# Denominator in two float32r parts from the second image on, with two-segment instructions, in a windowed-similarity kernel

## The chip, the cores and the metric

The kernel runs on one core of one Trainium2 chip. The metric is the device time of one execution in microseconds. The engines are TensorE (PE, with its weight loads shown as PEld), VectorE (DVE), ScalarE (ACT), GpSimd (POOL) and SyncE (SP), which here issues all the DMAs. All data are float32.

## What is computed

Two layers act on x of shape (2 images, 256 rows, 256 columns, 384 channels). Each layer normalises x by groups of 12 channels and adds a ratio of windowed sums (window 5 along the image's width, 20 along the channels):

```python
def layer(x):
    x_n = _gn(x)                              # G = 32, mean and variance over (H, W, C // G)
    s = box_sum(x_n, 2, 5)                    # width window
    num = box_sum(s * s, 3, 20)               # channel window
    d = box_sum(box_sum(x_n * x_n, 2, 5), 3, 20)
    denum = d * c1[None, None, :, None]       # c1: how many columns each width window holds
    return x + nan_to_num(num / denum, nan=1.0)
out = layer(layer(x))
```

The statistics of a layer's input must be known before the layer may begin on that image.

## The kernel before

The work falls into four phases, `PHASES`: layer 1 image 1, layer 1 image 2, layer 2 image 1, layer 2 image 2. The notes below and the prediction call them phases 0 to 3. A phase has 128 pairs of image rows (`NPAIR`), a tile has 8 rows (4 pairs), and a loop body has two tiles (8 pairs, `BODY`). Two `x_in` and two `y_out` buffers hold one tile each. One pair is four segments (`PSEG`) of 128 columns by 384 channels.

What each engine does for a pair p:

- POOL: `centre` (L312) subtracts the mean, two pairs ahead; `add_ratio` (L321) adds x to the finished ratio of the pair before.
- ACT: `squares` (L369, two halves, `Q0` and `Q1`); `take` (L385 and L388) moves a width sum out of PSUM, squared for the numerator (`sT`, steps `S`), copied and scaled for the denominator (`tT`, steps `T`); `invert` (L398 and L401, steps `L0` to `L3`) makes a reciprocal of a denominator segment as Exp(-Ln(d)).
- PE: `width_unit` (L468) multiplies the centred values (`S0` to `S2`) and the squares (`T0` to `T2`) by the width band, four matmuls of 130 output columns for each of three channel blocks, into three `width_ps` banks taken in turn. `channel_unit` (L492) multiplies `tT` (`D0` to `D3`, into three `den_ps` banks) or `sT` (`N0` to `N3`, into two `num_ps` banks) by the channel band, three matmuls of 138, 147 and 137 columns for each segment. In both the data are the stationary operand, so that each matmul in the code has a weight load.
- DVE: `approach` (L631) and `weigh` (L637) for each of the four segments, `divide` (L649) once for the pair (together one Newton step and the product), `measure_output` (L555, eight BATCH_NORM_STATS2 for each pair in phases 0 and 1, for layer 2's statistics) and `measure_beside` (L555, in phase 0, statistics of image 2: 3, 3 and 5 instructions in three of four pairs). `lane_totals` (L562) aggregates at a few places, eight or eleven instructions at a time.
- SP: for each tile the load of the tile after next, the store of the finished one, and in phase 0 the tile for `measure_beside`.

The order on each engine is written out by hand. PE works through the list below for each pair, where S and T belong to the next pair and D and N to the current one (F are three short parts in which the next phase's statistics are made, once in a phase). ACT's list is `S0 L0 T0 L1 S1 Q0 T1 L2 Q1 S2 T2 L3`. DVE's order is the body of `tiles`. Nothing reorders these lists, and an instruction that waits holds up all that stands behind it on its engine.

```python
for what in ("S0", "F1", "D0", "F2", "T0", "D1", "S1", "F3", "N0", "T1", "D2", "S2", "N1", "T2",
             "D3", "N2", "N3"):
```

Of the kernel before, what the change touches and what calls it, by code (L numbers as in the profile page):

```python
# [25 lines left out]
F32 = mybir.dt.float32  # L26
ACT = mybir.ActivationFunctionType
# [18 lines left out]
def similarity_layers_kernel(nc, x, out):  # L46
# [27 lines left out]

    def tiles_of(t, b):
        return t[b].rearrange("h (j p) c -> p (h j) c", p=P)
# [5 lines left out]
    with ExitStack() as ctx:  # L82
# [14 lines left out]
        newton = sb("newton", [P, PSEG, C])  # L97
        beside = sb("beside", [P, SEGS, C])
# [11 lines left out]
        band_c = [sb(f"band_c{k}", [P, c_span[k][1] - c_span[k][0]]) for k in range(KB)]  # L110
        identity = sb("identity", [P, P])
# [23 lines left out]
        width_taken = sem("width_taken")  # L135
        den_done = sem("den_done")
# [49 lines left out]
        with nc.Block() as block:  # L186
# [161 lines left out]
            def _(act):  # L348
# [13 lines left out]
                def squares(ph, p, par, half):  # L362
                    if half == 0:
                        act.wait_ge(rows_centred, ph * NPAIR + p + 1)
                        if not is_opening(ph, p, 2):

                            act.wait_ge(width_done, (ph * NPAIR + p - 1) * UNITS)
                    h = slice(half * 2, half * 2 + 2)
                    nc.scalar.activation(square[par][:, h, :], centred[par][:, h, :], ACT.Square  # L369
                                         ).then_inc(rows_squared, 1)  # L370

                def take(ph, p, par, k, is_t):

                    u = 2 * k + is_t
                    if u == 0:
                        if isinstance(p, int) and p == 0:

                            act.wait_ge(params_ready, ph + 1)
                        if not is_opening(ph, p, 2):

                            act.wait_ge(num_done, (ph * NPAIR + p - 1) * PSEG)
                    act.wait_ge(width_done, (ph * NPAIR + p) * UNITS + u + 1)
                    src = width_ps[u % 3][:]
                    if is_t:
                        nc.scalar.activation(tT[par][:, k, :], src, ACT.Copy, scale=rvar_col[ph][:, k:k + 1]  # L385
# [5 lines left out]
                def invert(ph, p, par, i):  # L391

                    base = ph * NPAIR
                    if i == 0 and not is_opening(ph, p, 2):

                        act.wait_ge(ratio_done, base + p - 1)
                    act.wait_ge(den_done, (base + p) * PSEG + i + 1)
                    nc.scalar.activation(recip[par][:, i, :], den_ps[i % 3][:, 0:C], ACT.Ln, bias=bias_ln[:],  # L398
                                         scale=LN_SCALE).then_inc(log_done, 1)
                    act.wait_ge(log_done, (base + p) * PSEG + i + 1)  # L400
                    nc.scalar.activation(recip[par][:, i, :], recip[par][:, i, :], ACT.Exp, bias=bias_exp[:],  # L401
                                         scale=-1.0).then_inc(recip_done, 1)

                def step(ph, p, par):

                    (ph1, p1), (ph2, p2) = in_phase(ph, p + 1), in_phase(ph, p + 2)
                    for what in ("S0", "L0", "T0", "L1", "S1", "Q0", "T1", "L2", "Q1", "S2", "T2", "L3"):
                        n = int(what[1])
                        if what[0] == "L":
                            invert(ph, p, par, n)  # L410
                        elif what[0] == "Q":
                            if ph2 < NP_:
                                squares(ph2, p2, par, n)
                        elif ph1 < NP_:
                            take(ph1, p1, 1 - par, n, int(what[0] == "T"))

                finish_logs(0)
                for p in range(2):
                    for half in range(2):
                        squares(0, p, p, half)  # L420
# [11 lines left out]
            def _(pe):  # L432
# [4 lines left out]
                def finish_part(ph, part):  # L437
# [3 lines left out]
                    if part < 3:  # L441
                        for half in range(2):
                            last = nc.tensor.matmul(num_ps[part - 1][:, 0:GROUPS], over_p[:],  # L443
                                                    stat_two[:, 2 * (part - 1), half, :],
                                                    start=(half == 0), stop=(half == 1))
                    else:
                        for k in range(KB):
                            last = nc.tensor.transpose(den_ps[2][:, P * k:P * (k + 1)],
# [3 lines left out]
                def width_unit(ph, p, par, k, is_t):  # L452
# [4 lines left out]
                    if u == 1:  # L457
                        pe.wait_ge(rows_squared, (ph * NPAIR + p + 1) * 2)
                    if not (is_opening(ph, p, 1) and u < 3):
# [4 lines left out]
                    bank = width_ps[u % 3]  # L464
# [8 lines left out]
                def channel_unit(ph, p, par, i, is_num):  # L473

                    seg = (ph * NPAIR + p) * PSEG + i
                    if i == 0 and not is_num:

                        pe.wait_ge(width_taken, (ph * NPAIR + p + 1) * UNITS)
                    if is_num:
                        bank, data = num_ps[i % 2], sT[par]  # L480
                        if not (is_opening(ph, p, 1) and i < 2):

                            pe.wait_ge(num_used, seg - 1)
                    else:
                        bank, data = den_ps[i % 3], tT[par]
                        if not (is_opening(ph, p, 1) and i < 3):

                            pe.wait_ge(den_used, seg if i == 0 else seg - 2 if i == 3 else seg - 3)
                    at = (i // 2) * W + (i % 2) * P
                    for k in range(KB):  # L490
                        lo, hi = c_span[k]
                        last = nc.tensor.matmul(bank[:, lo:hi], data[:, k, at:at + P], band_c[k][:],  # L492
# [272 lines left out]
```

## Time and profile before

| | us |
|---|---|
| median of 3 runs | 6088.27 |
| lowest and highest run | 6087.27, 6088.81 |
| span of the profiled execution | 6085.2 |
| PE busy | 5723.6 |
| ACT busy | 5014.0 |
| DVE busy | 4144.7 |
| POOL busy | 3546.7 |
| start of the first width matmul | 323.3 |

The first 311 us make the statistics of image 1 on DVE, with PE idle. From 323 us on PE runs, and the four phases follow one another without a break. The phase boundaries lie, by PE's work, near 1792, 3226 and 4656 us. Matmuls are pipelined, so the pitch from the start of one unit to the start of the next is its cost in a full stream, and the duration shown for one matmul is longer than that. On ACT and DVE too the next instruction may start some 0.1 us before the end of the one ahead of it.

### The profile page before, as it was taken

Reading aid. Unit: us, or ns where it says so; the run is one execution under the profiler, and the core shown is the slowest. Engines: PE = TensorE matmul, PEld = TensorE weight load, DVE = VectorE, ACT = ScalarE, POOL = GpSimd, SP = SyncE. Lnnn points to the kernel's source line nnn. Section 1 sums busy time; section 2 is a strip of 40 time slices with the busy share of each in tenths; the row PEclk is TensorE's granted clock in tenths of the full one; section 3 lists DMA queues with packets and bytes.
Section 4 is the critical chain, followed back from the end, with each engine's and each line's share of the span. In section 5 each row is a group of like instructions: output and inputs, shape, how many; then the busy total and the mean of one; then the engine's idle time right before and its main releaser. Section 6 shows DMA issues by size and latency. Waiting matters only on the chain.

```text
span 6085.2 us, 139173 instructions
## 1 busy us (share of the span) xinstructions
PE 5723.6 (94%) x49196; PEld 5710.7 (94%) x49196; DVE 4144.7 (68%) x9033; ACT 5014.0 (82%) x8201; POOL 3546.7 (58%) x1043
## 2 busy tenths in 40 slices
PE   0089999999999999999999999999999999999999
PEld 0089999999999999999999999999999999999999
DVE  9988889988877766767667555555555555555555
ACT  0078888888888888888888888888888888888888
POOL 0056665566556666666665666666666666666665
PEclk9999999999999999999999999999999999999999
DMA  9946655556633433434334344343434434343343
GB/s 367 367 157 212 223 207 191 207 203 215 220 125 125 151 138 134 156 124 153 137 135 147 132 147 143 129 160 124 159 130 141 149 124 165 124 153 137 135 154 124
DMA packets 660641, 1007.81 MB, mean 166 GB/s; under 512 B 5168, under 2 KB 660528, under 8 KB 660528
## 3 DMA queue, kind: packets, MB, share of 16 engines
q1 hardware_dynamic: 660528, 1006.65, 47.1%
q14 instruction: 85, 0.70, 0.0%
q8 instruction: 28, 0.46, 0.0%
HBM read 603.98 MB, written 402.65 MB: 165 GB/s over the span
## 4 chain that ended last, share of the span: by engine, by line
PE 89%; DVE 8%; issue 2%; ACT 1%; DMA 0%; SPq 0%; DVEq 0%; POOL 0%; POOLq 0%; ACTq 0%
PE width_ps L468 43%; PE den_ps L492 23%; PE num_ps L492 23%; DVE out_stats L555 3%; DVE lane_mv L562 2%; DVE y_out L649 1%; DVE newton L631 1%; DVE recip L637 0%; DMA y_out<-in_x_dram 0%; DVE beside_stats L555 0%; ACT recip L398 0%; ACT recip L401 0%; SPq L198 0%; DVEq L555 0%; PE num_ps L443 0%
## 5 line engine op out<-in xcount | busy, mean ns | idle before, releaser
L312 POOL TENSOR_TENSOR centred<-x_in,mean_row 128x1536 f32<-128x1536 f32 x512 | 1771.0, 3459 | 1415.0 <-PE width_ps L468 1097.5
L321 POOL TENSOR_TENSOR y_out<-x_in,y_out 128x1536 f32<-128x1536 f32 x512 | 1771.4, 3460 | 1117.1 <-DVE y_out L649 1117.1
L631 DVE SCALAR_TENSOR_TENSOR newton<-den_ps,recip 128x384 f32<-128x384 f32 x2048 | 1110.7, 553 | 1884.7 <-ACT recip L401 1854.8
L492 PE MATMUL den_ps<-band_c,tT 128*128 128x138 f32 (+2 forms) x12288 | 1809.0, 283 | 9.6 <-DVE newton L631 9.6
L492 PE MATMUL num_ps<-band_c,sT 128*128 128x138 f32 (+2 forms) x12288 | 1732.6, 284 | 20.4 <-DVE recip L637 20.1
L468 PE MATMUL width_ps<-band_w,centred 128*128 128x130 f32 x12288 | 1628.3, 275 | 0.5 <-DVE rvar_col L620 0.5
L468 PE MATMUL width_ps<-band_wc,square 128*128 128x130 f32 x12288 | 1625.5, 275 | 0.0
L492 PEld LDWEIGHTS den_ps<-band_c,tT 128*128 128x128 f32 x12288 | 1608.9, 190 | 13.3 <-DVE newton L631 11.8
L492 PEld LDWEIGHTS num_ps<-band_c,sT 128*128 128x128 f32 x12288 | 1580.5, 190 | 27.7 <-DVE recip L637 22.9
L388 ACT ACTIVATE sT<-width_ps,rstd_col 128x512 f32<-128x512 f32 x1536 | 1035.8, 674 | 592.9 <-PE width_ps L468 592.9
L468 PEld LDWEIGHTS width_ps<-band_w,centred 128*128 128x128 f32 x12288 | 1507.0, 191 | 0.9 <-DVE rvar_col L620 0.9
L468 PEld LDWEIGHTS width_ps<-band_wc,square 128*128 128x128 f32 x12288 | 1504.1, 191 | 0.0
L401 ACT ACTIVATE recip<-recip,bias_exp 128x384 f32<-128x384 f32 x2048 | 1260.4, 615 | 66.5
L398 ACT ACTIVATE recip<-den_ps,bias_ln 128x384 f32<-128x384 f32 x2048 | 1183.1, 578 | 64.7 <-PE den_ps L492 16.6
L637 DVE SCALAR_TENSOR_TENSOR recip<-num_ps,recip 128x384 f32<-128x384 f32 x2048 | 1085.0, 547 | 0.1
L385 ACT ACTIVATE tT<-width_ps,rvar_col 128x512 f32<-128x512 f32 x1536 | 1040.3, 677 | 2.6 <-PE width_ps L468 2.6
L649 DVE SCALAR_TENSOR_TENSOR y_out<-newton,recip 128x1536 f32<-128x1536 f32 x512 | 903.4, 1764 | 22.9
L369 ACT ACTIVATE square<-centred 128x768 f32<-128x768 f32 x1024 | 848.9, 829 | 3.7 <-POOL centred L312 3.7
L555 DVE BATCH_NORM_STATS2 out_stats<-y_out 128x192 f32 (+1 forms) x2560 | 689.7, 344 | 1.2 <-DMA y_out<-in_x_dram 1.0
L443 PE MATMUL num_ps<-stat_two,over_p 128*128 128x32 f32 x32 | 6.0, 319 | 313.7 <-DVE stat_two L584 312.8
L443 PEld LDWEIGHTS num_ps<-stat_two,over_p 128*128 128x128 f32 x32 | 5.4, 241 | 314.6 <-DVE band_wc L578 311.6
L555 DVE BATCH_NORM_STATS2 beside_stats<-beside 128x192 f32 (+1 forms) x960 | 273.6, 345 | 0.2
(44 smaller groups left out, 302.8 us busy)
## 6 DMA issues: line engine op xcount, KB each, us to landing
x_in<-in_x_dram SPq DMA_DIRECT2D x80, 3072.0 KB, 11.0
first_layer_out<-y_out SPq DMA_DIRECT2D x64, 3072.0 KB, 18.2
x_in<-first_layer_out SPq DMA_DIRECT2D x64, 3072.0 KB, 10.9
out_dram<-y_out SPq DMA_DIRECT2D x63, 3072.0 KB, 18.1
beside<-in_x_dram SPq DMA_DIRECT2D x30, 3072.0 KB, 11.0
y_out<-in_x_dram SPq DMA_DIRECT2D x18, 3072.0 KB, 24.4
out_dram<-y_out SPq DMA_DIRECT2D x4, 768.0 KB, 3.5
```

The costliest lines, as they stand in the source:

```text
L312: nc.gpsimd.tensor_tensor(centred[e % 2][:], x_in[slot][:, g * PSEG:(g + 1) * PSEG, :], mean_row[ph % 2][:].unsqueeze(1).to_broadcast([P, ...
L321: nc.gpsimd.tensor_tensor(y_out[slot][:, g * PSEG:(g + 1) * PSEG, :], x_in[slot][:, g * PSEG:(g + 1) * PSEG, :], y_out[slot][:, g * PSEG:( ...
L385: nc.scalar.activation(tT[par][:, k, :], src, ACT.Copy, scale=rvar_col[ph][:, k:k + 1]).then_inc(width_taken, 1)
L388: nc.scalar.activation(sT[par][:, k, :], src, ACT.Square, scale=rstd_col[ph][:, k:k + 1]).then_inc(width_taken, 1)
L398: nc.scalar.activation(recip[par][:, i, :], den_ps[i % 3][:, 0:C], ACT.Ln, bias=bias_ln[:], scale=LN_SCALE).then_inc(log_done, 1)
L401: nc.scalar.activation(recip[par][:, i, :], recip[par][:, i, :], ACT.Exp, bias=bias_exp[:], scale=-1.0).then_inc(recip_done, 1)
L468: last = nc.tensor.matmul(bank[:, at:at + WN], data[:, r * 2 + j, P * k:P * (k + 1)], band[:, j, :], start=(r == 0 and j == 0), stop=(r == ...
L492: last = nc.tensor.matmul(bank[:, lo:hi], data[:, k, at:at + P], band_c[k][:], start=(k == 0), stop=(k == KB - 1), skip_group_check=True)
L555: last = nc.vector.bn_stats(stats[:, g, bass.ds(column * 6, 6)], tile[:, :, CG * g:CG * (g + 1)])
L631: nc.vector.scalar_tensor_tensor(newton[:, i, :], den_ps[i % 3][:, 0:C], TINY, recip[par][:, i, :], ALU.add, ALU.mult).then_inc(den_used, 1)
L637: nc.vector.scalar_tensor_tensor(recip[par][:, i, :], num_ps[i % 2][:, 0:C], TINY, recip[par][:, i, :], ALU.add, ALU.mult).then_inc(num_us ...
L649: nc.vector.scalar_tensor_tensor(y_out[slot][:, g * PSEG:(g + 1) * PSEG, :], newton[:], 2.0, recip[e % 2][:], ALU.subtract, ALU.mult).then ...
```

## The change

From phase 1 on (`SPLIT_FROM = 1`) the denominator's width sums are kept as two float32r tensors. ACT's `take` writes `t_top` (L385's place), a value rounded to float32r. A new DVE instruction, `rest`, computes the sum once more from the same PSUM bank and subtracts `t_top`, which gives `t_rest`. PE multiplies both by a float32r band, so that a D unit has six matmuls in the code in place of three. The band's spans begin on even columns: 138, 148 and 138 columns. Phase 0 keeps `tT` and its float32 band. Further:

- `width_ps` has two banks, one for S and one for T. T units wait for `rest` of the T unit before them (`rest_taken`).
- `den_ps` has two pairs of banks and `num_ps` one pair. `invert`, `approach` and `weigh` take two segments in one instruction, and `squares` takes the whole pair. ACT's list becomes `S0 T0 L0 S1 T1 Q S2 T2 L1`.
- `newton` is gone; `approach` writes into `y_out`, and so it now waits for the store of the earlier tile (`out_landed`), which `divide` did.
- D2 and N1 change places in PE's list.
- The new tensors take the memory of `beside`, which is not used after phase 0.

```diff
+    r_span = [(lo - lo % 2, hi) for lo, hi in c_span]
+    SPLIT_FROM = 1
...
-        width_ps = [ctx.enter_context(nc.psum_tensor(f"width_ps{i}", [P, 2 * W], F32)) for i in range(3)]
-        den_ps = [ctx.enter_context(nc.psum_tensor(f"den_ps{i}", [P, 512], F32)) for i in range(3)]
-        num_ps = [ctx.enter_context(nc.psum_tensor(f"num_ps{i}", [P, 512], F32)) for i in range(2)]
+        width_ps = [ctx.enter_context(nc.psum_tensor(f"width_ps{i}", [P, 2 * W], F32)) for i in range(2)]
+        den_ps = [ctx.enter_context(nc.psum_tensor(f"den_ps{i}", [P, 2, 512], F32)) for i in range(2)]
+        num_ps = ctx.enter_context(nc.psum_tensor("num_ps", [P, 2, 512], F32))
...
+                    both = recip[par][:, 2 * h:2 * h + 2, :]
+                    nc.scalar.activation(both, den_ps[h][:, :, 0:C], ACT.Ln, bias=bias_ln[:],
                                          scale=LN_SCALE).then_inc(log_done, 1)
...
-                    for what in ("S0", "L0", "T0", "L1", "S1", "Q0", "T1", "L2", "Q1", "S2", "T2", "L3"):
+                    for what in ("S0", "T0", "L0", "S1", "T1", "Q", "S2", "T2", "L1"):
...
-                        pe.wait_ge(width_taken, (ph * NPAIR + p) * UNITS + u - 2)
+                        pe.wait_ge(width_taken, (ph * NPAIR + p) * UNITS + u - 1)
+                    if is_t and ph >= SPLIT_FROM and not (ph == SPLIT_FROM and isinstance(p, int) and p + k == 0):
+
+                        pe.wait_ge(rest_taken, ((ph - SPLIT_FROM) * NPAIR + p) * KB + k)
...
+                        lo, hi = r_span[k]
+                        for part in (t_top[par], t_rest[par]):
+                            last = nc.tensor.matmul(bank[:, lo:hi], part[:, k, at:at + P], band_r[k][:],
+                                                    start=(k == 0 and part is t_top[par]),
+                                                    stop=(k == KB - 1 and part is t_rest[par]),
+                                                    skip_group_check=True)
...
+                def rest(ph, p, par, k):
...
+                    dve.wait_ge(width_taken, unit)
+                    nc.vector.scalar_tensor_tensor(t_rest[par][:, k, :], width_ps[1][:], rvar_col[ph][:, k:k + 1],
+                                                   t_top[par][:, k, :].bitcast(F32), ALU.mult, ALU.subtract
+                                                   ).then_inc(rest_taken, 1)
...
+                            if splits:
+                                rest(ph1, p1, 1 - par, 0)
+                            approach(ph, p, par, 0, i, lo, e)
+                            measure_beside(ph, i, lo, e, 0)
+                            if splits:
+                                rest(ph1, p1, 1 - par, 1)
                             weigh(ph, p, par, 0)
+                            measure_beside(ph, i, lo, e, 1)
+                            if splits:
+                                rest(ph1, p1, 1 - par, 2)
+                            approach(ph, p, par, 1, i, lo, e)
+                            measure_beside(ph, i, lo, e, 2)
                             weigh(ph, p, par, 1)
...
+                            divide(ph, p, e)
                             measure_output(ph, i, lo, e)
```

## Rows read from the trace of the kernel before

**Rows 1.** The page: engines, and shares of the last chain by engine and line.
```profile
PE 5723.6 (94%) x49196; PEld 5710.7 (94%) x49196; DVE 4144.7 (68%) x9033; ACT 5014.0 (82%) x8201; POOL 3546.7 (58%) x1043
PE 89%; DVE 8%; issue 2%; ACT 1%; DMA 0%; SPq 0%; DVEq 0%; POOL 0%; POOLq 0%; ACTq 0%
```

**Rows 2.** The last chain in order of time (start, length, what), one pair in phase 2.
```profile
4009.96 1.44 PE num_ps L492 x12
4011.40 0.89 PE width_ps L468 x8
4012.29 0.72 PE den_ps L492 x6
...
4021.08 1.44 PE num_ps L492 x12
```

**Rows 3.** Busy time by stretch: PE, PEld, DVE, ACT, POOL, granted clock, DMA share, GB/s.
```profile
2080.00:3180.00 1100.00, 1098.59 (x9466) 1096.66 (x9465) 778.01 (x1712) 965.57 (x1579) 681.99 (x198) 1.00 0.40 141
3330.00:4600.00 1270.00, 1269.69 (x10965) 1269.53 (x10964) 668.03 (x1028) 1118.53 (x1830) 791.72 (x230) 1.00 0.41 144
```

**Rows 4.** PE in time order, phase 2: narrow matmuls and the transposes.
```profile
3320.72 0.63 PE L443 MATMUL num_ps<-stat_two,over_p 128*128 128x32 f32 x4 [0.59 <-DVE stat_two L584]
3321.19 0.96 PE L492 MATMUL den_ps<-band_c,tT 128*128 128x138 f32 x6
...
3325.25 0.49 PE L448 MATMUL den_ps<-identity,rstd_row 128*128 128x128 f32 x3
3325.57 0.88 PE L492 MATMUL num_ps<-band_c,sT 128*128 128x138 f32 x6
```

**Rows 5.** Groups by line: busy us, mean ns, then idle before, of DVE and ACT.
```profile
L631 DVE SCALAR_TENSOR_TENSOR newton<-den_ps,recip 128x384 f32<-128x384 f32 x2048 | 1110.7, 553 | 1884.7 <-ACT recip L401 1854.8 <-issue 2.1 <-DVE y_out L649 0.5
L649 DVE SCALAR_TENSOR_TENSOR y_out<-newton,recip 128x1536 f32<-128x1536 f32 x512 | 903.4, 1764 | 22.9
L401 ACT ACTIVATE recip<-recip,bias_exp 128x384 f32<-128x384 f32 x2048 | 1260.4, 615 | 66.5
L398 ACT ACTIVATE recip<-den_ps,bias_ln 128x384 f32<-128x384 f32 x2048 | 1183.1, 578 | 64.7 <-PE den_ps L492 16.6
L385 ACT ACTIVATE tT<-width_ps,rvar_col 128x512 f32<-128x512 f32 x1536 | 1040.3, 677 | 2.6 <-PE width_ps L468 2.6
L369 ACT ACTIVATE square<-centred 128x768 f32<-128x768 f32 x1024 | 848.9, 829 | 3.7 <-POOL centred L312 3.7
L359 ACT ACTIVATE stat_tmp<-stat_tmp,bias_rstd 128x32 f32<-128x32 f32 x4 | 1.3, 321 | 0.1
L356 ACT ACTIVATE stat_tmp<-stat_tmp,bias_var 128x32 f32<-128x32 f32 x4 | 1.3, 322 | 329.0 <-DVE stat_tmp L605 329.0
```

**Rows 6.** ACT in time order, phase 2: the pitch of takes, Ln and Exp.
```profile
4003.07 0.67 ACT L385 ACTIVATE tT<-width_ps,rvar_col 128x512 f32<-128x512 f32 x1
4003.64 0.57 ACT L398 ACTIVATE recip<-den_ps,bias_ln 128x384 f32<-128x384 f32 x1
4004.24 0.62 ACT L401 ACTIVATE recip<-recip,bias_exp 128x384 f32<-128x384 f32 x1
```

**Rows 7.** DVE in time order: aggregations of phase 0; a pair's end in phase 1.
```profile
1676.58 5.05 DVE L562 BATCH_NORM_AGGREGATE lane_mv<-beside_stats 128x2 f32<-128x96 f32 x11
...
2077.31 1.01 DVE L637 SCALAR_TENSOR_TENSOR recip<-num_ps,recip 128x384 f32<-128x384 f32 x2
2078.46 1.76 DVE L649 SCALAR_TENSOR_TENSOR y_out<-newton,recip 128x1536 f32<-128x1536 f32 x1
2080.14 2.17 DVE L555 BATCH_NORM_STATS2 out_stats<-y_out 128x192 f32 x8
2082.22 1.00 DVE L631 SCALAR_TENSOR_TENSOR newton<-den_ps,recip 128x384 f32<-128x384 f32 x2
```

**Rows 8.** PE in time order around two waits, end of phase 0.
```profile
1667.98 1.45 PE L492 MATMUL num_ps<-band_c,sT 128*128 128x138 f32 x6 [3.66 <-DVE recip L637]
1669.22 1.94 PE L468 MATMUL width_ps<-band_w,centred 128*128 128x130 f32 x8
1670.95 1.29 PE L492 MATMUL den_ps<-band_c,tT 128*128 128x138 f32 x6
1672.08 1.06 PE L468 MATMUL width_ps<-band_wc,square 128*128 128x130 f32 x8
...
1683.52 0.99 PE L492 MATMUL num_ps<-band_c,sT 128*128 128x138 f32 x6 [2.49 <-DVE recip L637]
1684.34 1.06 PE L468 MATMUL width_ps<-band_w,centred 128*128 128x130 f32 x8
```

**Rows 9.** Stretches as in Rows 3: behind the longer wait, behind the shorter.
```profile
1669.20:1671.00 1.80, 1.80 (x10) 1.80 (x10) 1.80 (x7) 0.00 (x0) 0.00 (x0) 0.50 0.00 0
1684.00:1690.00 6.00, 6.00 (x55) 6.00 (x54) 5.97 (x16) 4.47 (x8) 1.20 (x1) 1.00 0.00 1
```

**Rows 10.** DMA queue's issues in time order; the page's landing time.
```profile
516.58 1.63 SPq L253 DMA_DIRECT2D first_layer_out<-y_out  x1
first_layer_out<-y_out SPq DMA_DIRECT2D x64, 3072.0 KB, 18.2
```

More of the change, by code:

```diff
@@ L26 @@
 F32 = mybir.dt.float32
+F32R = mybir.dt.float32r
 ACT = mybir.ActivationFunctionType
@@ L96, in similarity_layers_kernel @@
         recip = [sb(f"recip{i}", [P, PSEG, C]) for i in range(2)]
-        newton = sb("newton", [P, PSEG, C])
-        beside = sb("beside", [P, SEGS, C])
+        with nc.sbuf_tensor("beside", [P, SEGS, C], F32) as beside:
+            pass
+        t_top = [sb(f"t_top{i}", [P, KB, 2 * W], F32R) for i in range(2)]
+        t_rest = [sb(f"t_rest{i}", [P, KB, 2 * W], F32R) for i in range(2)]
         out_stats = sb("out_stats", [P, GROUPS, SPLIT * 6])
@@ L110, in similarity_layers_kernel @@
         band_c = [sb(f"band_c{k}", [P, c_span[k][1] - c_span[k][0]]) for k in range(KB)]
+        band_r = [sb(f"band_r{k}", [P, r_span[k][1] - r_span[k][0]], F32R) for k in range(KB)]
         identity = sb("identity", [P, P])
@@ L360, in finish_logs, with squares @@
                                          scale=-0.5).then_inc(log_given, 1)
[L362 to L370, printed above, removed]
+                def squares(ph, p, par):
+                    act.wait_ge(rows_centred, ph * NPAIR + p + 1)
+                    if not is_opening(ph, p, 2):
+                        act.wait_ge(width_done, (ph * NPAIR + p - 1) * UNITS)
+                    nc.scalar.activation(square[par][:], centred[par][:], ACT.Square).then_inc(rows_squared, 1)
                 def take(ph, p, par, k, is_t):
@@ L411, in step @@
                         elif what[0] == "Q":
                             if ph2 < NP_:
-                                squares(ph2, p2, par, n)
+                                squares(ph2, p2, par)
                         elif ph1 < NP_:
-                            take(ph1, p1, 1 - par, n, int(what[0] == "T"))
+                            take(ph1, p1, 1 - par, int(what[1]), int(what[0] == "T"))
                 finish_logs(0)
                 for p in range(2):
-                    for half in range(2):
-                        squares(0, p, p, half)
+                    squares(0, p, p)
@@ L479, in channel_unit @@
                     if is_num:
[L480 to L488 removed]
+                        bank, data = num_ps[:, i % 2, :], sT[par]
@@ L489, in channel_unit @@
+                        if i % 2 == 0 and not (is_opening(ph, p, 1) and h == 0):
+                            pe.wait_ge(num_used, pair * 2 + h)
+                    else:
+                        bank, data = den_ps[h][:, i % 2, :], tT[par]
+                        if i % 2 == 0 and not is_opening(ph, p, 1):
+                            pe.wait_ge(den_used, pair * 2 + h - 1)
                     at = (i // 2) * W + (i % 2) * P
                     for k in range(KB):
-                        lo, hi = c_span[k]
@@ L492, in channel_unit @@
[L492 to L494 removed]
+                        if is_num or ph < SPLIT_FROM:
+                            lo, hi = c_span[k]
+                            last = nc.tensor.matmul(bank[:, lo:hi], data[:, k, at:at + P], band_c[k][:],
+                                                    start=(k == 0), stop=(k == KB - 1), skip_group_check=True)
+                            continue
@@ L579, in _ @@
                                                        float(REACH + 1 + d), None, ALU.mult)
+                for k in range(KB):
+                    lo, hi = r_span[k]
+                    at = c_span[k][0] - lo
+                    if at:
+                        nc.vector.tensor_scalar(band_r[k][:, 0:at], band_c[k][:, 0:at], 0.0, None, ALU.mult)
+                    last = nc.vector.tensor_copy(band_r[k][:, at:], band_c[k][:])
                 last.then_inc(bands_ready, 1)
@@ new lines, in weigh, with divide @@
+                def weigh(ph, p, par, h):
+                    dve.wait_ge(num_done, (ph * NPAIR + p) * 2 + h + 1)
+                    both = recip[par][:, 2 * h:2 * h + 2, :]
+                    nc.vector.scalar_tensor_tensor(both, num_ps[:, :, 0:C], TINY, both, ALU.add, ALU.mult
+                                                   ).then_inc(num_used, 1)
+                def divide(ph, p, e):
+                    slot, g = e // PAIRS, e % PAIRS
+                    dve.wait_ge(num_used, (ph * NPAIR + p + 1) * 2)
+                    dve.wait_ge(den_used, (ph * NPAIR + p + 1) * 2)
+                    near = y_out[slot][:, g * PSEG:(g + 1) * PSEG, :]
+                    nc.vector.scalar_tensor_tensor(near, near, 2.0, recip[e % 2][:], ALU.subtract, ALU.mult
+                                                   ).then_inc(ratio_done, 1)
```

99 lines of the change are left out of this document (43 added, 56 removed).

## The prediction

> **What bounds the kernel now.** I read the page's engine line and the chain that ended last first [rows 1]: PE is busy 94% of the span and holds 89% of the chain. The chain in order of time [rows 2] shows one pair from the start of its `N2 N3` (x12) to the next: 11.12 us. A width unit takes 0.895 us there (0.89 and 0.90 alternate), a channel unit 0.72, and 6 x 0.895 + 8 x 0.72 = 11.13, so that the period of a pair is PE's own work. The stretches of phases 1 and 2 [rows 3] leave PE idle 1.4 us of 1100 and 0.3 of 1270 at a granted clock of 1.00 (2.4 GHz); ACT is busy 88% there, DVE 71% and 53%. So PE work saved is worth its full time until another limit comes, and the next limit need not be one engine's sum: it can be a circle of waits.
>
> **PE work removed.** A width unit's four matmuls appear as eight records and take 0.895 us [rows 2], 224 ns for each matmul of 130 columns; four streams of 130 columns at 2.4 GHz are 217. A float32 matmul thus costs four streams plus some 1.8 ns for each. If a float32r matmul is one stream, a D unit of six matmuls of 141 columns on average is 6 x (141.3/2.4 + 1.8) = 0.37 us, and saves 0.35. No float32r matmul is in the trace. Upper bounds: the narrow matmuls at L443, 32 columns wide, follow each other at (3321.19 - 3320.72)/4 = 0.12 us, and the three transposes of 128 columns, one record each, at (3325.57 - 3325.25)/3 = 0.107 [rows 4]; by these a matmul with its own weight load or with a 4-byte stream costs 0.11, and a D unit 0.66. If float32r takes four streams as float32 does, it is 1.43. Below 0.37 there is nothing, as no record streams faster than the clock. I take 0.37, near the count of streams the diff is about, and keep 0.66 and 1.43.
>
> The Trainium skill (FP8 and Floating Point Precision, TensorE Precision Notes) says true FP32 needs four passes and that the reduced form reads 4 bytes and truncates; the first agrees with the 224 ns, the second is in no trace here. Against the change speaks TensorE: Matmul & The Clock Gate, LDWEIGHTS: a load costs P/1.2, 107 ns for 128 columns, which would make a D unit 0.64; the spacing of 0.12 behind the narrow matmuls agrees with it, and it is a rival below.
>
> **What is added to DVE and ACT.** DVE: from 384 to 1536 elements one instruction grows from 553 to 1764 ns [rows 5], 1.05 ns for an element. A `rest` (512) is then 0.69 us, 0.61 in pitch; a wide `approach` or `weigh` (768) 0.955, 0.875 in pitch (the pitch is some 0.08 below the duration: two `weigh` in 1.01 us [rows 7]). `divide` has pitch 1.68 and eight statistics 2.08 [rows 7]. ACT: Ln grows from 322 (32 elements) to 578 (384), 0.73 ns an element, Exp from 321 to 615, 0.84 [rows 5]; from squares against takes (152 ns for 256) I would get 0.6. With 0.71 and 0.78 a wide Ln is 0.85, a wide Exp 0.91, a whole square 1.38, a take 0.57 in pitch [rows 6]. Sums for a pair: ACT 6 x 0.57 + 2 x (0.88 + 0.81) + 1.28 = 8.1 us; DVE in phases 2 and 3 1.8 + 3.5 + 1.7 = 7.0, in phase 1 9.1; PE 11.13 - 4 x 0.35 = 9.73. By sums PE would still bound, at 9.73.
>
> **The new circle.** By waits it doesn't. `T1` of the next pair waits for `rest` 0; that stands on DVE behind the previous pair's `divide` and, in phase 1, behind its statistics; these stand behind `weigh` 1 and `approach` 1, which needs the reciprocal of `D3`; and `D3` stands on PE behind that pair's own `T1`. Round it once, with 0.03 us for each hand-over (Ln ends at 4003.64 + 0.57 = 4004.21 and Exp, which needs it, starts at 4004.24 [rows 6]): `rest` 0 0.72; `T1 N1 S2 D2 T2` 0.895 + 0.72 + 0.895 + 0.37 + 0.895 = 3.78; the end of the last matmul and hand-over 0.20; take `T2` 0.57; Ln 0.88; Exp 0.94; `approach` 0.875; `weigh` 0.985 (the next waits for its end); `divide` 1.68. Sum 10.62 us. Phases 2 and 3 run at that, 0.50 under 11.12. In phase 1 the eight statistics are in the circle: 12.70, 1.58 over. What waits behind T1 is all of PE: N1, S2, D2 and so on.
>
> **By phase.** Phase 0: D is unchanged. Two segments in an instruction save DVE little, but `approach` 1 now begins only after a wide Ln and Exp behind `D3`, and with 5 + 8 statistics and two wide instructions behind it `weigh` 0 comes some 0.4 us late for `N2` in the pairs with `measure_beside`; the fourth pair gives most back. I take +18, between 0 and +40. Phase 1: 128 x 1.58 = +202, and the 64 aggregations of 0.46 us (eleven in 5.05 [rows 7]) no longer lie partly beside PE, +23 net: +225. Phase 2: -0.50 x 128 = -64, while the statistics and aggregations of its first four pairs cost 24: -40. Phase 3: -62. Start: five small DVE instructions for the band, 1 (an estimate; eight statistics of 192 elements take 2.08). Sum: +142, and 5 for work between phases, +147. Against the profiled 6085.2 this is 6232; the median lies 3.1 above that execution, so 6235 us. The 0.03 hand-overs and the wide ACT slope are the soft terms: 0.2 us in the circle is 77 us over 384 pairs.
>
> **What costs nothing.** `approach` waits for the store where `divide` did, some 5 us earlier; a store is issued at 516.58 and lands 18.2 later [rows 10], at 535, while the next tile for that buffer begins, one body of 89 us after the last, near 549. The cover is 14 us; were it gone, DVE would wait at one pair in four with PE behind it. The memory that takes `beside`'s place is written long after its last use. Load order on SP is untouched. POOL's two instructions, 6.9 us a pair, keep their slack. D2 behind N1 moves D2's end by nothing that ACT waits for.
>
> **Rivals.** (1) The weight load or the 4-byte stream sets the pace, D = 0.66 to 0.72: D2 and D3 are both in the circle then (`D3` ends after the take), 11.00 and 13.08 us: phases 2 and 3 gain 16 each, phase 1 loses 275. With 18 and 30 for the rest: some 6380, to 6430 at 0.72. (2) Four streams for each float32r matmul, D = 1.43: PE alone needs 11.13 + 4 x 0.71 = 13.97, 2.85 over in phases 2 and 3 and, with the circle, 3.7 over in phase 1: 6088 + 730 + 480 + 40 = 7340. For it: nothing shows that 138 columns stream any faster; against: the transposes do half the float32 records' streams. (3) The clock falls. In phase 1 PE stands still 12.70 - 9.73 = 2.97 us in each pair. Behind an idle stretch of 3.66 us the clock was 0.50 and N, W and D took 1.24, 1.73 and 1.13 in place of 0.72, 0.895 and 0.72, 1.77 more; behind 2.49 us it stayed at 1.00 [rows 8, 9]. 2.97 lies between. If each pair paid it, all of it in the circle: 128 x 1.8 = +230, 6465 us; if half did, 6350. (4) Faster: the circle is shorter than my sum. The wide Ln, Exp, `approach` and `weigh` are 3.7 of its 10.6 us and all extrapolated. If the second segment costs only two thirds of what I take, the circle loses 0.6 us: 6235 - 384 x 0.6 = 6005. It decides from 0.38 us a pair (147/384). At the far end PE's sum sets all three phases: 6088 + 20 - 384 x 1.39 = 5575.
>
> **How the numbers follow.** Forecast, one stream, clock held: 0.38. Clock lost in many pairs of phase 1: 0.15. Rival 1: 0.16. Rival 2: 0.13. Rival 4: 0.14, most of it near 6005, and 0.04 between it and the forecast that ends within 0.2% (12 us, what a measurement of this kernel can tell from no change). Faster 0.14, same 0.04, slower 0.82. The range 6020 to 6480 leaves out rival 2 and the far half of rival 4, 0.2 in all.
>
> **What would show it.** Right: chain rows with a D unit of 0.37; the x12 rows 10.6 us apart in phases 2 and 3, 12.7 in phase 1; PE waiting for `rest` at T1, some 0.9 and 2.9 us each; the last chain shared by PE, DVE and ACT. Wrong: periods of 9.7 with no such wait (rival 4), D rows of 0.66 (rival 1), two records for each float32r matmul (rival 2), a granted clock under 1.00 between 1810 and 3450 us (rival 3), or DVE waiting for a store at `approach`.

## The result, and the profile after

The changed kernel takes 6557.94 us (median of 4 runs, 6557.03 to 6558.8) against 6087.77; the ratio is 1.077, 95% interval 1.076 to 1.079. The forecast was 6235 us, range 6020 to 6480: slower, as forecast, but by three times as much, and outside the range. The first view is the page of the profile: busy time of the engines, and then three of its groups of instructions (busy us, mean ns of one, then the idle time before them and what ended it).

```profile
PE 5837.1 (89%) x49196; PEld 5744.3 (88%) x49196; DVE 4783.3 (73%) x8142; ACT 4543.0 (69%) x5641; POOL 3550.6 (54%) x1043
...
L475 PE MATMUL width_ps<-band_wc,square 128*128 128x130 f32 x12288 | 1737.6, 285 | 347.9 <-DVE t_rest L657 336.3
...
L657 DVE SCALAR_TENSOR_TENSOR t_rest<-width_ps,rvar_col,t_top 128x512 fp32r<-128x512 f32 x1152 | 861.3, 748 | 1000.9 <-ACT t_top L391 1000.5
...
L508 PEld LDWEIGHTS den_ps<-band_r,t_rest 128*128 128x128 f32 x4608 | 883.7, 192 | 0.0
```

PE is busy 89% where it was 94% [rows 1], and is not less busy in microseconds: 5837 for 5724. Its count of instructions is the same, 49196: a float32 matmul appears as two records, a float32r one as one, and there are twice as many of the latter. 336 us of idle time stand ahead of the T units and end with `t_rest`.

The chain that ended last, one pair of phase 2 (start, length, what), answers [rows 2]:

```profile
4503.01 1.49 PE num_ps L503 x12
4504.50 0.89 PE width_ps L475 x8
4505.39 0.62 PE den_ps L508 x6
4506.02 0.94 PE width_ps L475 x8
4506.96 0.62 PE den_ps L508 x6
4507.58 0.94 PE width_ps L475 x8
4508.52 0.72 PE num_ps L503 x6
4509.24 0.04 issue
4509.28 1.16 PE width_ps L475 x8
...
4514.24 1.49 PE num_ps L503 x12
```

The pair takes 11.23 us, where it took 11.12. A D unit and the width unit behind it are 0.62 + 0.94 = 1.56 us, against 0.72 + 0.895 = 1.615 before: D costs 0.67, not 0.37. T1 starts at 4509.28, at a hand-over, and takes longer than the others. The same place in phase 1, PE and then DVE in order of time:

```profile
2404.49 1.10 PE L475 MATMUL width_ps<-band_w,centred 128*128 128x130 f32 x8
2405.43 0.88 PE L503 MATMUL num_ps<-band_c,sT 128*128 128x138 f32 x6
2408.43 1.16 PE L475 MATMUL width_ps<-band_wc,square 128*128 128x130 f32 x8 [2.12 <-DVE t_rest L657]
```

```profile
2402.90 0.95 DVE L679 SCALAR_TENSOR_TENSOR recip<-num_ps,recip 128x768 f32<-128x768 f32 x1
2403.88 1.76 DVE L689 SCALAR_TENSOR_TENSOR y_out<-y_out,recip 128x1536 f32<-128x1536 f32 x1
2405.55 2.17 DVE L574 BATCH_NORM_STATS2 out_stats<-y_out 128x192 f32 x8
2407.64 0.73 DVE L657 SCALAR_TENSOR_TENSOR t_rest<-width_ps,rvar_col,t_top 128x512 fp32r<-128x512 f32 x1
```

`weigh`, `divide`, the statistics and `rest` 0 follow each other without a gap, and T1 starts 0.06 us behind the end of `rest` 0. That is the circle of the prediction, at work in every split pair of phase 1. In the pairs with aggregations T1 waits longer, 6.0 us in place of 2.12: eight aggregations stand ahead of `rest` 0 as well.

From the starts of `N2 N3` (x12), pair by pair, a table by phase. The periods are those of the long even stretches; a length goes from the last pair of the phase before to the last pair of the phase itself (for phase 0 from its first pair, for phase 3 to the one before its last):

| phase | length before | length after | period before | period after | forecast period |
|---|---|---|---|---|---|
| 0 | 1449.8 | 1482.0 | 11.12 | 11.12 to 11.40 | 11.26 |
| 1 | 1434.5 | 1800.8 | 11.12 | 13.31, one in five 14.9 to 15.0 | 12.70 |
| 2 | 1430.0 | 1485.3 | 11.12 | 11.24 | 10.62 |
| 3 | 1411.8 | 1427.2 | 11.12 | 11.24 | 10.62 |

The differences are 32, 366, 55 and 15 us, 469 of the 472 between the spans (6557.1 and 6085.2).

### The profile page after: what moved, and what is told of

The parts are those of the page before. It is cut to its first block and busy times, and to the rows that moved or that the text cites. A ratio compares the mean times of both kernels' runs of the same rounds, so it can differ in the third digit from the quotient of the medians.

```text
span 6557.1 us, 134037 instructions
## 1 busy us (share of the span) xinstructions
PE 5837.1 (89%) x49196; PEld 5744.3 (88%) x49196; DVE 4783.3 (73%) x8142; ACT 4543.0 (69%) x5641; POOL 3550.6 (54%) x1043
## 5 line engine op out<-in xcount | busy, mean ns | idle before, releaser
L657 DVE SCALAR_TENSOR_TENSOR t_rest<-width_ps,rvar_col,t_top 128x512 fp32r<-128x512 f32 x1152 | 861.3, 748 | 1000.9 <-ACT t_top L391 1000.5
L671 DVE SCALAR_TENSOR_TENSOR y_out<-den_ps,recip 128x768 f32<-128x768 f32 x1024 | 977.8, 955 | 715.0 <-ACT recip L408 711.8
L508 PE MATMUL den_ps<-band_r,t_top 128*128 128x138 f32 (+1 forms) x4608 | 1166.9, 287 | 0.0
L508 PE MATMUL den_ps<-band_r,t_rest 128*128 128x138 f32 (+1 forms) x4608 | 1110.8, 275 | 0.0
L408 ACT ACTIVATE recip<-recip,bias_exp 128x768 f32<-128x768 f32 x1024 | 958.7, 936 | 33.1
L679 DVE SCALAR_TENSOR_TENSOR recip<-num_ps,recip 128x768 f32<-128x768 f32 x1024 | 969.6, 947 | 4.9 <-PE num_ps L503 4.9
L405 ACT ACTIVATE recip<-den_ps,bias_ln 128x768 f32<-128x768 f32 x1024 | 923.5, 902 | 11.8 <-PE den_ps L508 3.6
L689 DVE SCALAR_TENSOR_TENSOR y_out<-y_out,recip 128x1536 f32<-128x1536 f32 x512 | 900.5, 1759 | 17.5
L508 PEld LDWEIGHTS den_ps<-band_r,t_rest 128*128 128x128 f32 x4608 | 883.7, 192 | 0.0
L508 PEld LDWEIGHTS den_ps<-band_r,t_top 128*128 128x128 f32 x4608 | 881.0, 191 | 0.0
L375 ACT ACTIVATE square<-centred 128x1536 f32<-128x1536 f32 x512 | 754.9, 1474 | 3.8 <-POOL centred L320 3.8
```

The lines of the kernel that those rows point to most:

```text
L405: nc.scalar.activation(both, den_ps[h][:, :, 0:C], ACT.Ln, bias=bias_ln[:], scale=LN_SCALE).then_inc(log_done, 1)
L408: nc.scalar.activation(both, both, ACT.Exp, bias=bias_exp[:], scale=-1.0).then_inc(recip_done, 1)
L508: last = nc.tensor.matmul(bank[:, lo:hi], part[:, k, at:at + P], band_r[k][:], start=(k == 0 and part is t_top[par]), stop=(k == KB - 1 an ...
L657: nc.vector.scalar_tensor_tensor(t_rest[par][:, k, :], width_ps[1][:], rvar_col[ph][:, k:k + 1], t_top[par][:, k, :].bitcast(F32), ALU.mul ...
L671: nc.vector.scalar_tensor_tensor(y_out[slot][:, at:at + 2, :], den_ps[h][:, :, 0:C], TINY, recip[par][:, 2 * h:2 * h + 2, :], ALU.add, ALU ...
L679: nc.vector.scalar_tensor_tensor(both, num_ps[:, :, 0:C], TINY, both, ALU.add, ALU.mult).then_inc(num_used, 1)
```

## The experiments

My theory after the result (theory A in the expectations): the circle `rest` 0, T1, D3, reciprocal, `divide`, `rest` 0 is right; D = 0.67 makes it longer and takes the gain away, because each float32r matmul needs a weight load of 0.11 us. Rivals: the two-segment instructions or the two width banks cost by themselves (theory B); PE loses time between float32 and float32r; DVE's sum of work bounds (theory C); it is the stream of float32r (theory H), not its load (theory L), that is slow. Five of the kernels below were timed once only: statistics behind `rest` 0, `rest` 0 ahead of `divide`, two banks, wide band and narrow rest. What they show rests on their periods, which repeat within 0.01 us from pair to pair in the even stretches, more than on their totals.

**No split.** The wide instructions, banks and orders alone.

```diff
-    SPLIT_FROM = 1
+    SPLIT_FROM = 4
```

> The changed kernel with SPLIT_FROM = 4: no phase is split, so that only the two-segment instructions, the two width banks and the new orders on PE and ACT are left. Theory A (the loss comes from the circle T1 <- rest 0 <- divide and statistics, which exists only in split phases): phases 1 to 3 return to a period of 11.12 us, phase 0 keeps its 32 us loss, total 6088 + 35 = 6120 us (6105 to 6140). Theory B (the wide Ln, Exp, approach and weigh, or two width banks in place of three, cost by themselves wherever they stand): phases 2 and 3 stay at 11.2 or more and phase 1 well above 12, total 6250 us or more.

Measured: 6127.86 us, ratio 1.0065 (1.005 to 1.008). Phases 1 to 3 are back at 11.12 (lengths 1441, 1434, 1412), phase 0 keeps its loss, 1478.7 against 1449.8. So the rest of the change costs 40 of the 470 us by itself, and the split, put on top of it, 430. Theory B, that the two-segment instructions or the two banks cost the time wherever they stand, falls; what they cost together with the split is seen below, under two banks.

**Statistics behind rest 0.** For seven of eight pairs.

```diff
                                 rest(ph1, p1, 1 - par, 0)
+                            if e > 0:
+                                measure_output(ph, i, lo, e - 1)
                             approach(ph, p, par, 0, i, lo, e)
...
                             divide(ph, p, e)
-                            measure_output(ph, i, lo, e)
+                            if e == BODY - 1:
+                                measure_output(ph, i, lo, e)
```

> The changed kernel with the statistics of a pair moved on DVE from behind divide to behind the next pair's rest 0 (for seven of eight pairs). Theory A: the eight statistics (2.08 us) leave the circle of phase 1, which is then held by T2 <- rest 1 at about 12.0 to 12.3 in the mean; 6558 - 128 x 1.5, and without the lost clock another 40 less: 6320 us (6290 to 6380). The granted clock in phase 1 goes back to 1.00, since PE's longest wait falls from 2.1 us to below 1. Theory B (two-segment instructions by themselves): no change, 6558. Theory C (DVE's sum of work bounds phase 1): no change either, as DVE does the same work.

Measured: 6322.03 us. In phase 1 most periods are 11.66 in place of 13.31, with the same DVE work; phases 2 and 3, which have no statistics, stay at 11.24. The stretch from 2000 to 2600 us (PE, PEld, DVE, ACT, POOL, clock, DMA share, GB/s), here and then in the changed kernel from 2000 to 2700:

```profile
2000.00:2600.00 600.00, 574.83 (x4833) 557.99 (x4832) 478.46 (x812) 444.76 (x555) 349.80 (x101) 1.00 0.39 136
```

```profile
2000.00:2700.00 700.00, 591.74 (x4938) 581.37 (x4937) 489.31 (x819) 454.83 (x566) 353.72 (x103) 0.98 0.33 117
```

DVE's share of the time rises from 70% to 80%, which an engine that bounds by its work couldn't do. Three of the 24 periods there are over 1.6 us longer, one behind each pair whose statistics were not moved. T1 waits 2.12 us in them, as in the changed kernel. Two take 13.31 us at a granted clock of 1.00, which is the old circle and nothing else, and one takes 14.94 at a mean clock of 0.89. So the lower clock too is seen only where that wait is.

**Rest 0 ahead of divide**, for the pair after next, so that neither `divide` nor statistics stand in the circle.

```diff
-                            if splits:
-                                rest(ph1, p1, 1 - par, 0)
                             approach(ph, p, par, 0, i, lo, e)
...
+                            if SPLIT_FROM <= ph2 < NP_:
+                                rest(ph2, p2, par, 0)
                             divide(ph, p, e)
```

> The changed kernel with rest 0 of the pair after next put ahead of divide on DVE, so that T1 waits for neither divide nor statistics. Theory A: phases 2 and 3 fall to PE's own sum 6 x 0.895 + 4 x 0.67 + 4 x 0.72 = 10.93 us a pair from 11.24; phase 1 is then held by T2 <- rest 1, 12.6; total 6558 - 80 - 128 x 1.4 = about 6300 to 6370 us. If instead PE has costs between float32 and float32r units that no wait explains, phases 2 and 3 stay at 11.1 to 11.2.

Measured: 6363.57 us. The chain in phase 3:

```profile
5002.54 0.94 PE width_ps L475 x8
5003.49 0.72 PE num_ps L503 x6
5004.21 0.90 PE width_ps L475 x8
5005.10 0.72 PE num_ps L503 x6
5005.82 0.89 PE width_ps L475 x8
```

T1 (at 5004.21) starts where N0 ends, and N1 follows 0.90 us behind its start, where it was 1.00 in the changed kernel (4509.28 to 4510.28). Phases 2 and 3 run at 10.93 us, PE's own sum with D at 0.67, so that no other cost of float32r is left to find. Phase 1 runs at 12.57 for the most part (T2 behind `rest` 1, which stands behind the statistics), 12.6 expected.

**Three banks.** The kernel before with the split alone: one-segment instructions, three width banks in turn, `approach` into `y_out`.

```diff
+                    if ph >= SPLIT_FROM and not is_t and not (ph == SPLIT_FROM and isinstance(p, int) and
+                                                              p == 0 and k < 2):
+
+                        pe.wait_ge(rest_taken, ((ph - SPLIT_FROM) * NPAIR + p) * KB + k - 1)
...
-                            approach(ph, p, par, 0)
-                            approach(ph, p, par, 1)
...
+                            if splits:
+                                rest(ph1, p1, 1 - par, 0)
+                            approach(ph, p, par, 0, i, lo, e)
+                            approach(ph, p, par, 1, i, lo, e)
+                            if splits:
+                                rest(ph1, p1, 1 - par, 1)
                             weigh(ph, p, par, 0)
```

> The kernel before with only the split added: one-segment instructions, three width banks, PE's and ACT's old orders; approach writes into y_out to make room in memory. A rest has until two width units later to free its bank (S2 waits for rest 0, not T1). Theory A: PE's sum bounds phases 1 to 3 at 10.93 us, phase 0 is as in the kernel before; 6088 - 384 x 0.19 = 6015 us (6000 to 6035), faster than both kernels. Rival (the split costs PE or ACT time of its own beyond the 0.67 of a D unit): phases 2 and 3 at 11.1 or more, 6080 us or more. Rival (DVE's sum, 10.2 us in phase 1, binds in some other order): phases 2 and 3 at 10.93 but phase 1 at 11.5 or more, 6090 us.

Measured: 6080.93 us, ratio 0.9987 (0.9978 to 0.9996), 0.1% faster than before but 66 us over my number. The even stretches of phases 1 to 3 are at 10.93 as expected. What I had not reckoned with are three groups of four pairs with aggregations, at 16.3 to 17.7 us each. One of them, DVE and then PE:

```profile
1824.35 2.17 DVE L579 BATCH_NORM_STATS2 out_stats<-y_out 128x6 f32<-128x192 f32 x8
1826.56 3.72 DVE L586 BATCH_NORM_AGGREGATE lane_mv<-out_stats 128x2 f32<-128x96 f32 x8
1830.31 0.75 DVE L662 SCALAR_TENSOR_TENSOR t_rest<-width_ps,rvar_col,t_top 128x512 fp32r<-128x512 f32 x1
```

```profile
1831.11 2.10 PE L481 MATMUL width_ps<-band_w,centred 128*128 128x130 f32 x8 [3.51 <-DVE t_rest L662]
1833.01 1.61 PE L509 MATMUL num_ps<-band_c,sT 128*128 128x138 f32 x6
```

The eight aggregations stand ahead of `rest` 0, and S2 waits 3.51 us for it. S2 and the unit behind it then show 2.10 and 1.61 us, where such rows show 1.06 to 1.11 and 0.88 in the even stretches. The granted clock there:

```profile
1831.10:1834.40 3.30, 3.29 (x14) 3.29 (x15) 2.48 (x5) 0.69 (x1) 0.00 (x0) 0.50 0.00 0
```

So a wait and a clock at the lower of its two levels (1.2 GHz) come together.

**Two banks** in that kernel, one for S and one for T as in the change; T1 waits for `rest` 0 again.

```diff
-        width_ps = [ctx.enter_context(nc.psum_tensor(f"width_ps{i}", [P, 2 * W], F32)) for i in range(3)]
+        width_ps = [ctx.enter_context(nc.psum_tensor(f"width_ps{i}", [P, 2 * W], F32)) for i in range(2)]
...
-                    bank = width_ps[u % 3]
+                    bank = width_ps[u % 2]
```

> The three-bank kernel (one-segment instructions, split from phase 1) with two width banks, one for S and one for T, as in the changed kernel, so that T1 waits for rest 0 again. Theory A (the bank decides which unit waits for rest 0): phase 1 falls back to about 12.2 us a pair, since rest 0 stands behind divide and the statistics; phases 2 and 3 stay at 10.93, because with one-segment Ln and Exp the circle without statistics is shorter than PE's sum; total about 6250 us. If the bank count doesn't matter: 6081.

Measured: 6278.51 us, phase 1 at 12.33, phases 2 and 3 at 10.93. The one bank is worth 198 us (one run against the median of the three-bank kernel), through the unit that it makes wait:

```profile
2205.94 1.16 PE L480 MATMUL width_ps<-band_wc,square 128*128 128x130 f32 x8 [1.14 <-DVE t_rest L661]
```

The changed kernel has these two banks and the same split, and takes 279 us more (6557.94 against 6278.51; 13.31 against 12.33 in phase 1, 11.24 against 10.93 in phases 2 and 3). What is left between the two kernels are the two-segment instructions and the orders on PE and ACT. They cost 40 us without the split; it is in the circle that they are dear, where Ln, Exp and `approach` take 902, 936 and 955 ns for two segments in place of 578, 615 and 553 for one. No run parts the wide instructions from the orders.

**Wide band.** The float32r band filled with zeros to 384 columns.

```diff
-    r_span = [(lo - lo % 2, hi) for lo, hi in c_span]
+    r_span = [(0, C) for lo, hi in c_span]
```

> The changed kernel with the float32r band filled up with zeros to 384 columns, so that each of the six matmuls of a D unit streams 384 columns in place of 138 to 148, with the same weight loads. If a float32r matmul streams one column a clock and it is the weight load that sets the 0.11 us of each (theory L), one takes 384/2.4 + 2 = 0.162 us, a D unit 0.97, PE's sum 12.13 us in phases 2 and 3, and the total about 6880 us. If float32r streams at half that rate and this sets the 0.11 us (theory H), one takes 0.32 us, a D unit 1.93, PE's sum 15.97, and the total about 8100 us.

Measured: 6923.92 us; phases 2 and 3 at 12.44. PE in order of time:

```profile
5400.55 0.34 PE L508 MATMUL den_ps<-band_r,t_rest 128*128 128x384 f32 x1
5400.73 0.34 PE L508 MATMUL den_ps<-band_r,t_top 128*128 128x384 f32 x1
5400.90 0.34 PE L508 MATMUL den_ps<-band_r,t_rest 128*128 128x384 f32 x1
```

A matmul of 384 columns follows the last one by 0.175 us, at a granted clock of 1.00: 160 ns are its columns at 2.4 GHz, and 15 are left unexplained (I had expected 2). Six of them make D 1.05 and PE's sum 12.45, which agrees with the period of 12.44. The stream is near one column a clock, and theory H (half that rate, 0.32) falls.

**Narrow rest.** The matmuls of `t_rest` cut to 64 columns.

```diff
-                            last = nc.tensor.matmul(bank[:, lo:hi], part[:, k, at:at + P], band_r[k][:],
+                            n = hi - lo if part is t_top[par] else 64
+                            last = nc.tensor.matmul(bank[:, lo:lo + n], part[:, k, at:at + P], band_r[k][:, 0:n],
```

> The changed kernel with the matmuls of t_rest cut to the first 64 columns of each span (the low part of the other columns is left out), those of t_top whole. Theory L (the weight load sets the 0.11 us): nothing changes, a D unit stays at 0.67 and the total at 6558 us. Theory H (the stream sets it): the narrow ones take 0.055 us, a D unit 0.52, and with D2 and D3 in the circle the total falls to about 6450 us.

Measured: 6549.94 us, phases 2 and 3 at 11.20. The weight loads, in order of time, and the matmuls of the same unit:

```profile
5400.92 0.19 PEld L509 LDWEIGHTS den_ps<-band_r,t_rest 128*128 128x128 f32 x1
5401.03 0.19 PEld L509 LDWEIGHTS den_ps<-band_r,t_top 128*128 128x128 f32 x1
5401.15 0.19 PEld L509 LDWEIGHTS den_ps<-band_r,t_rest 128*128 128x128 f32 x1
5401.26 0.19 PEld L509 LDWEIGHTS den_ps<-band_r,t_top 128*128 128x128 f32 x1
```

```profile
5400.99 0.24 PE L509 MATMUL den_ps<-band_r,t_rest 128*128 128x64 f32 x1
5401.06 0.32 PE L509 MATMUL den_ps<-band_r,t_top 128*128 128x148 f32 x1
5401.21 0.24 PE L509 MATMUL den_ps<-band_r,t_rest 128*128 128x64 f32 x1
```

The matmuls start 0.07 and 0.15 apart by turns, but a pair of them still takes 0.22, and the loads come every 0.11, whatever the width of what follows. Cutting half of the matmuls to less than half of their columns gives 8 us of 6558. The weight load sets the price. All loads here are of 128 columns, so no run tells whether the 0.11 us goes with the columns loaded or is a fixed price of a load with its matmul.

**Late aggregations.** The three-bank kernel with the 32 aggregations of each place spread, five a pair, over seven pairs and put behind `rest` 0.

```diff
-                    if ends:
-                        dve.wait_ge(stats_done, tile * PAIRS + q + 1)
-                        lane_totals(*ends, quarter, out_stats)
+                def late_totals(ph, lo, e, part):
...
+                    done = 5 * (e - 1) + 2 * part
+                    groups = range(max(0, done), min(GROUPS, done + (2 if part < 2 else 1)))
+                    if e > 0 and len(groups):
+                        dve.wait_ge(stats_done, tile * PAIRS + groups[-1] // chunk + 1)
+                        lane_totals(*ends, groups, out_stats)
```

> The three-bank kernel with the 32 aggregations at each of three places no longer eight at a time behind the statistics of four pairs, but five a pair over seven pairs, behind rest 0. Theory A (in those twelve pairs rest 0 stands behind divide, statistics and aggregations, S2 waits 3.5 us for it, and the clock falls): the twelve pairs of 16.3 to 17.3 us become pairs of 10.9 to 12.7, total 6040 us (6025 to 6055). If instead DVE's sum of work bounds these stretches, the same work takes as long wherever it stands: 6070 us or more.

Measured: 6026.48 us (6025.87 to 6027.08), ratio 0.990 (0.988 to 0.992). This version beats both kernels, the one before by 62 us and the changed one by 531. Its page:

```profile
PE 5651.2 (94%) x49196; PEld 5637.4 (94%) x49196; DVE 4918.2 (82%) x10190; ACT 4954.6 (82%) x8201; POOL 3553.6 (59%) x1043
```

PE is at its own sum again, 72 us less busy than in [rows 1], and all the other engines have more to do than in the changed kernel or as much. It is the wait that was taken away, not work: the twelve pairs of 16.3 to 17.7 us are gone, those with aggregations take 12.2 to 12.3 us for the most part, and the even stretches stay at 10.93. The mean granted clock of the run is 0.999, where it was 0.992 with the waits of 3.5 us.

**Weigh first.** The kernel without split, with `weigh` 0 ahead of the first three statistics of image 2 in phase 0.

```diff
-                            measure_beside(ph, i, lo, e, 0)
                             if splits:
                                 rest(ph1, p1, 1 - par, 1)
                             weigh(ph, p, par, 0)
+                            measure_beside(ph, i, lo, e, 0)
```

> The changed kernel without any split (as the first experiment, 6128 us) and with weigh 0 ahead of the first three statistics of image 2 on DVE in phase 0. Theory A (phase 0 loses because weigh 0 comes late for N2: behind two-segment approach 1, five statistics, weigh 1, divide, eight statistics, approach 0 and three statistics): 0.78 us less stand ahead of it, the periods of phase 0 of 11.2 to 11.4 go back to 11.12, total 6105 us (6098 to 6112). If the two-segment instructions cost PE in another way in phase 0, nothing changes: 6128.

Measured: 6102.51 us, ratio 1.0025 (1.0015 to 1.0034), 25 us less than without it. So most of what phase 0 loses is `weigh` 0 coming late for N2, as argued. Of the 15 us that stay over the kernel before, by the same lengths as in the table, 3 lie in phase 0 (1453.0 against 1449.8), 8 in phase 1 and 4 in phase 2; their cause was not looked for.

## Why the prediction was wrong, point by point

**What bounds, and the circle: right.** PE was the bound before and a circle of waits takes its place; T1 behind `rest` 0 behind `divide` and the statistics was named with its members. Three experiments take members out and the period follows: 13.31 to 11.66 without the statistics, 11.24 to 10.93 without `divide`, 12.33 to 10.93 (three banks for two) with another unit waiting. T1's wait, forecast at 0.9 and 2.9 us, is 0.24 (4509.28) and 2.12 us, since four D units of 0.67 fill 1.2 us more of the pair.

**The price of a D unit: the step that failed.** I counted streams of columns and took 0.37 us; it is 0.67. The rows for the right number stood in front of me [rows 4]. The transposes, one record and one load each, came every 0.107 us, where the count of streams would give them 0.055. And the four records at L443 are two float32 matmuls of two records each, not four matmuls as I read them; but each record has its own load, and 0.12 us for a record of 32 columns can't be bound by the columns. I kept that as an upper bound and as rival 1 at 0.16, and took the count of streams because the diff speaks of it. The wide and the narrow band show both halves: the stream is indeed near one column a clock, and the load of 0.11 us hides it at 64 to 148 columns (up to some 230 by an estimate from 0.11 us, 2.4 GHz and the 15 ns of the wide band; no run has a width between 148 and 384). The sentence of the Trainium skill (TensorE: Matmul & The Clock Gate, LDWEIGHTS) that a load takes P/1.2 ns for P columns, 107 ns for 128, agrees with loads every 0.11 us here; it should have had the forecast, not a rival's place. The split saves 4 x 0.05 us of PE's time a pair and not 4 x 0.35.

**The circle's length: 0.2 short.** By rival 1 with its own D, phases 2 and 3 should have run at 11.00 and phase 1 at 13.08; they run at 11.24 and 13.31. Of the 0.24, `rest` is 0.748 for 0.69, Ln 0.902 for 0.85, Exp 0.936 for 0.91, D 0.67 for 0.66 twice, and T1 itself 0.1 longer (from 4509.28 to N1 at 4510.28 it is 1.00 for 0.895). Its first weight load has nothing to hide under: load and matmul both start at 4509.28, where the load for N1 starts at 4510.17, 0.11 ahead of its matmul. Together 0.26. Each is small and all have one sign; I had 0.2 as a soft term, but beside the forecast's case only, not added to the rival's.

**The clock: half right.** I asked whether an idle stretch of 2.97 us, between the 2.49 and 3.66 us of [rows 8], would lower it. PE idles 2.12 us by the profile in each pair of phase 1, and one pair in five has a granted clock of 0.51 behind that wait, and lasts 14.9 to 15.0 us. The same 3.2 us behind two such waits, the first with the clock lost:

```profile
2243.70:2246.90 3.20, 3.20 (x14) 3.20 (x15) 1.19 (x2) 1.12 (x2) 0.71 (x1) 0.51 0.33 52
2230.40:2233.60 3.20, 3.20 (x29) 3.20 (x29) 2.09 (x3) 2.04 (x3) 0.69 (x1) 1.00 0.00 0
```

So 2.49 us without a loss [rows 8] was no safe side: a shorter wait loses it too, now and then. It costs 1.65 us in a fifth of the pairs, 128 x 0.34 = 44 us. The pairs with aggregations lose more: behind waits of 6.0 us all twelve have a mean clock of 0.82 or 0.83. They are 74 us longer than twelve pairs of 13.31; 12 x 3.9 = 47 of these are the longer wait, and the 27 that are left are what the clock costs there (an estimate).

**Phase 1 summed:** 128 x (13.31 - 11.12) = 280, the clock 44, the two places with aggregations 47 over an even stretch at the mean period of 13.66 (19.76 + 20.06 + 18.62 + 19.52 - 4 x 13.66 = 23 at the first, 23 at the second), the making of the next phase's statistics 7, less 12 that the kernel before lost at the same places: 366, as measured. I had 225.

**Phases 0, 2 and 3.** Phase 0 was forecast at +18 in 0 to 40 and is +32. Phase 2 was -40 and is +55, phase 3 -62 and is +15: with a period of 11.24 both signs turn. The period makes only 15 us in each. The other 40 of phase 2 are its first pair at the lower clock (4), its four pairs with aggregations (33) and the making of the next statistics (10), less 7 that the kernel before lost there; I had 24 for all of it.

**What costs nothing: right.** No row of DVE waiting for a store stands among the changed kernel's waits, and the three-bank kernel, which has the same early wait in `approach`, runs at PE's sum in its even stretches.

**The range.** Rival 1 was priced at 6380 to 6430 and rival 3 at up to 230 more, each alone. Both came, rival 3 for a part of its price, and the first with terms that were all somewhat short; the range was made from single cases and left no room for two. Of the 323 us between forecast and result, D's price makes 0.38 x 384 = 146, the rest of the circle's length 0.23 x 384 = 88, the clock of the even stretch 44, the pairs with aggregations and statistics some 35 and phase 0 14: within 4 us of the whole (an estimate from the lengths and periods above).

## What to carry to other kernels

Price a matmul by the larger of its stream and its weight load: when a change replaces few streams of a stationary operand by more loads, look in the trace for the narrowest matmuls and for those of one record, whose spacing shows what a load costs. Before a consumer is added to a buffer, write down which unit must wait for it and what is queued ahead of the consumer on its engine: here a third bank (198 us), or a place ahead of `divide` (194 us), was worth more than the arithmetic saved (4 x 0.05 x 384 = 77 us). And what an instruction for two segments costs depends on who waits for it: with the orders that go with it, at most 40 us without the split and 279 with it. Bursts of side work belong behind the instruction that frees a buffer, not ahead of it.

## What the runs showed of the hardware

- A float32r matmul is one record and one stream: 384 columns every 0.175 us at a granted clock of 1.00. At 138 to 148 columns, and with every second one cut to 64, one comes every 0.11 us in the mean, the spacing of the weight loads (128 columns each). A load lasts as long (0.19 us) as that of a float32 matmul.
- A granted clock of 0.51 behind an idle time of PE of 2.12 us, in one of five like pairs, where the same idle time left it at 1.00 in the other four.
- The first unit of eight records behind a wait takes 1.00 us in place of 0.895, at a granted clock of 1.00 (4509.28 and 2230.36 in the changed kernel).
- ACT's Ln and Exp on 768 elements took 902 and 936 ns, for 578 and 615 on 384 [rows 5]: 0.84 ns for each further element; `Square` 1474 for 1536 and 829 for 768, also 0.84. The 0.71 and 0.78 that I took were too low.
